# Another placement of the pair products in a CIN layer-1/layer-2 pipeline: steps 1, 6, 11, 16, 21, 26 and one group two tiles ahead

## The chip, the cores and the metric

The kernel runs on one core of one Trainium2 chip. The metric is the device time of one execution in microseconds (us). A core has five engines that run their own instruction streams and meet at semaphores: TensorE (PE, its weight loads are shown as PEld), VectorE (DVE), ScalarE (ACT), GpSimd (POOL) and SyncE (SP, which issues most DMAs here).

## The reference

For 1024 samples, 39 embedding rows of 16 numbers are gathered. Three layers of a compressed interaction network follow, and a small perceptron on their sums:

```
z   = einsum('bfd,bgd->bfgd', x0, xk).reshape(b, f * g, d)     # x0: 39 fields, xk: the layer before
cur = einsum('bpd,pm->bmd', z, W)                              # 128 outputs per layer, xk = cur
...
z = sum over d of the three cur, concatenated (384) and dense_ctx (16)
h = max(z @ W_top1 + b_top1, 0); h = max(h @ W_top2 + b_top2, 0); y = h @ W_top3
```

In layer 1 the pair (f, g) and the pair (g, f) share a product, so the kernel forms 20 shifted products of x with itself instead of 39 x 39.

## The kernel before, in words

**Tiles, blocks, quads.** The batch is cut into 32 tiles of 32 samples. A tile is 4 blocks of 8 samples (128 columns of sample x dimension). Four tiles make a quad, 8 quads in all: the first quad is written out, quads 1 to 6 are a hardware loop (`Fori`), and the last is written out. The four tiles of a quad are called the first to the fourth tile here (i = 0 to 3 in the code).

**Steps.** Each engine's program counts steps s = 0 to 39 in a tile, ten to a block (n = block, q = s % 10). In step s, PE makes one piece of layer 2 (`layer2_piece`: three matmuls, since fp32 is split in a high and a low part) in one of five PSUM banks (`pieces`). Pieces of even q are weighed by ACT (`weigh_piece`, four activations into `parts`), pieces of odd q by DVE (`sum_piece`, four, or three at q = 9, multiply-adds onto `parts`). PE may not reuse a bank before the piece of five steps earlier has been taken: step 10 waits for the DVE piece of step 5, and so on. When a block's 19 DVE multiply-adds are done, POOL adds its 20 partial sums in three instructions (`add_parts`: L342 over 1024 columns, L344 and L347 over 512), after the two or three gathers that its program has in front of them. DVE ends the addition one block later (`halve_tails` at q = 7, `finish_cur2` at q = 8).

**Layer 1 of the next tile.** It is put between these steps. It has seven groups k = 0 to 6 (`PAIRK`) per tile. For a group DVE multiplies `partners` by `x_rep` into one of two `pairs` buffers (`make_pairs`, L538, the product) at the step in `S_PAIR`. ACT takes the high part one step later (`take_pairs_high`, `S_HIGH`), DVE the low part two steps later (`take_pairs_low`, L554, `S_LOW`), and PE adds the group onto `cur1_bank` with three matmuls seven steps later (`sum_pairs`, L670 to L672, `S_SUM`). One and two steps after the last sum ACT and DVE take `cur1` out of PSUM (`copy_cur1_hi`, `take_cur1`). The product and the low part have all operands in SBUF; the multiply-adds of L528 read PSUM.

**Other work.** In the first and second tile of a quad PE also does layer 3 and the perceptron of the quad before (steps 25 to 55 of the quad). SP stores the gathered rows, loads `x_rep` and `partners` two tiles ahead and `x_diag` one tile ahead, in program order in one queue.

Of the kernel before, what the change touches and what calls it, by code (L numbers as in the profile page):

```python
# [32 lines left out]
TILES, BLOCKS = 4, 16  # L33
# [7 lines left out]
PAIRK = (SHIFTS + REP - 1) // REP  # L41
# [5 lines left out]
PIECES = 10  # L47
# [7 lines left out]

S_PAIR = [3 + 4 * k for k in range(PAIRK)]
S_HIGH = [x + 1 for x in S_PAIR]
S_LOW = [x + 2 for x in S_PAIR]  # L60
S_SUM = [x + 7 for x in S_PAIR]
S_G = [2, 12, 22, 32]
# [24 lines left out]
def cin_kernel(nc, t, out):  # L87

    ctx = ExitStack()
    with ctx:  # L90
# [291 lines left out]
        def _(act):  # L382
            def weigh_piece(u, n, q):

                g, i = u * BLOCKS + n, A_PIECES.index(q)
                k = g * len(A_PIECES) + i
                if i == 0:
                    wait(act, tree_done, (g - 1) * TREE)
                    act.wait_ge(x_cols_ready, u * TILES + n // 4 + 1)
                act.wait_ge(l2a_ready, k + 1)  # L390
                src = pieces[(n * PIECES + q) % BANKS]
                for r in range(4):
                    f = 4 * q + r
                    last = nc.scalar.activation(parts[n % 2][:, 4 * i + r, :], src[:, r * H:(r + 1) * H], ACT.Copy,  # L394
                                                scale=x_cols[n // 4][:, n % 4, f:f + 1])
                last.then_inc(prod_done, 1)
# [12 lines left out]
            def take_pairs_high(tile, i, k):  # L409
                g, buf, rows = tile * PAIRK + k, (i * PAIRK + k) % 2, rows_of(k)  # L410
                act.wait_ge(pairs_ready, g + 1)
                wait(act, pairs_used, g - 1)
                nc.scalar.activation(pairs_hi[buf][0:rows, :], pairs[buf][0:rows, :], ACT.Copy  # L413
                                     ).then_inc(pairs_hi_ready, 1)
# [45 lines left out]
            for part, cols in w1_raw:  # L460
                last = nc.scalar.activation(w1_hi[:, cols], part.rearrange("p f m -> p (f m)"), ACT.Copy)
# [12 lines left out]
            def quad(u, first, last):  # L474
                for i in range(TILES):
                    tile, more = u * TILES + i, not (last and i == TILES - 1)
                    for s in range(4 * PIECES):
                        n, q = 4 * i + s // PIECES, s % PIECES
                        if q in A_PIECES:
                            weigh_piece(u, n, q)  # L480
                        if more and s in S_HIGH:
                            take_pairs_high(tile + 1, i + 1, S_HIGH.index(s))
                        if more and s == S_X[i] + 1:
                            copy_x_cols(tile + 1, (i + 1) % TILES)
                        if s - 1 in (S_G_FIRST if i == 0 else S_G):
                            if n >= G_LAG:
                                copy_g(u, n - G_LAG)
                            elif not first:
                                copy_g(u - 1, BLOCKS + n - G_LAG)
                        at = 4 * PIECES * i + s  # L490
                        if not first:
                            if at == S_L3_COPY:
                                copy_l3(u - 1)
                            if at in S_RELU1:
                                relu1(u - 1, S_RELU1.index(at))
                            if at == S_RELU2:
                                relu2(u - 1)
                            if at - 1 == S_Y:
                                copy_y(u - 1)
                        if more and s == S_SUM[-1] + 1:  # L500
                            copy_cur1_hi(tile + 1, i + 1)
# [13 lines left out]
        def _(dve):  # L515
# [98 lines left out]
            def quad(u, first, last):  # L614
                for i in range(TILES):
                    tile, more = u * TILES + i, not (last and i == TILES - 1)
                    for s in range(4 * PIECES):
                        n, q = 4 * i + s // PIECES, s % PIECES
                        if q in D_PIECES:
                            sum_piece(u, n, q)  # L620
                        if q in (Q_HALVE, Q_FINISH):
                            step = halve_tails if q == Q_HALVE else finish_cur2
                            if n >= 2:
                                step(u, n - 2)
                            elif not first:
                                step(u - 1, BLOCKS + n - 2)
                        if more and s in S_PAIR:
                            make_pairs(tile + 1, i + 1, S_PAIR.index(s))
                        if more and s in S_LOW:
                            take_pairs_low(tile + 1, i + 1, S_LOW.index(s))  # L630
                        if more and s == S_SUM[-1] + 2:
                            take_cur1(tile + 1, (tile + 1) * TILE_B, i + 1)

# [242 lines left out]
```

## Time and profile before

| what | value |
|---|---|
| median of 3 runs (1337.85 to 1340.86) | 1338.43 us |
| profiled execution: its own time | 1340.8 us |
| profiled execution: span | 1339.0 us |
| granted TensorE clock, mean | 0.990 |
| PE busy | 1281.1 us, 96% of the span |
| DVE busy | 1149.6 us, 86% |
| POOL busy | 1058.3 us, 79% |
| ACT busy | 915.3 us, 68% |

The busy time of PE counts overlapping matmuls once, and the ends of matmuls are modelled, so 96% does not say by itself that PE sets the time. The shares are means over a quad whose four tiles are not alike.

### The profile page before, as it was taken

Reading aid. Unit: us, or ns where it says so; the run is one execution under the profiler, and the core shown is the slowest. Engines: PE = TensorE matmul, PEld = TensorE weight load, DVE = VectorE, ACT = ScalarE, POOL = GpSimd, SP = SyncE. Lnnn points to the kernel's source line nnn. Section 1 sums busy time; section 2 is a strip of 40 time slices with the busy share of each in tenths; the row PEclk is TensorE's granted clock in tenths of the full one; section 3 lists DMA queues with packets and bytes.
Section 4 is the critical chain, followed back from the end, with each engine's and each line's share of the span. In section 5 each row is a group of like instructions: output and inputs, shape, how many; then the busy total and the mean of one; then the engine's idle time right before and its main releaser. Section 6 shows DMA issues by size and latency. Waiting matters only on the chain. (4 is left out here: it accounts for less than half of the span.)

```text
span 1339.0 us, 25654 instructions
## 1 busy us (share of the span) xinstructions
PE 1281.1 (96%) x5983; PEld 1017.3 (76%) x5983; DVE 1149.6 (86%) x3210; ACT 915.3 (68%) x3053; POOL 1058.3 (79%) x743
## 2 busy tenths in 40 slices
PE   4899999999999999999999999999999999999998
PEld 2577777877788777887768877788767887788787
DVE  3499999699888999789986999969998699988983
ACT  2377776677666777577765777757776577766783
POOL 7588888688886888779887788868888688884561
PEclk9699999999999999999999999999999999999999
DMA  7623233322233322223332133330333322333000
GB/s 197 158 54 52 61 64 65 61 41 53 48 61 61 64 54 46 44 56 61 65 65 44 25 63 66 65 63 9 62 64 66 61 40 44 55 61 61 2 3 1
DMA packets 129470, 76.62 MB, mean 57 GB/s; under 512 B 90792, under 2 KB 98201, under 8 KB 129301
## 3 DMA queue, kind: packets, MB, share of 16 engines
q1 hardware_dynamic: 119061, 72.07, 26.5%
q0 software_dynamic: 10240, 2.64, 2.2%
q8 instruction: 64, 1.05, 0.3%
q14 instruction: 105, 0.86, 0.2%
HBM read 68.16 MB, written 3.87 MB: 54 GB/s over the span
## 5 line engine op out<-in xcount | busy, mean ns | idle before, releaser
L394 ACT ACTIVATE parts<-pieces,x_cols 128x128 f32<-128x128 f32 x2560 | 717.9, 377 | 188.3 <-PE pieces L690 159.4
L528 DVE SCALAR_TENSOR_TENSOR parts<-pieces,x_cols,parts 128x128 f32<-128x128 f32 x2432 | 678.7, 339 | 136.8 <-PE pieces L690 99.4
L688 PE MATMUL pieces<-w_hi,cur_hi 128*128 128x512 f32 (+1 forms) x1280 | 549.3, 429 | 29.2 <-DVE parts L528 23.0
L690 PE MATMUL pieces<-w_hi,cur_lo 128*128 128x512 f32 (+1 forms) x1280 | 499.4, 390 | 0.0
L689 PE MATMUL pieces<-w_lo,cur_hi 128*128 128x512 f32 (+1 forms) x1280 | 499.1, 390 | 0.0
L342 POOL TENSOR_TENSOR parts<-parts 128x1024 f32<-128x1024 f32 x127 | 324.2, 2553 | 149.8 <-DVE parts L528 144.4
L333 POOL DMA_INDIRECT emb<-in_table,rows x320 | 345.1, 1079 | 79.7 <-issue 60.9
L688 PEld LDWEIGHTS pieces<-w_hi,cur_hi 128*128 128x128 f32 x1280 | 242.1, 189 | 102.3 <-DVE parts L528 46.4
L690 PEld LDWEIGHTS pieces<-w_hi,cur_lo 128*128 128x128 f32 x1280 | 241.2, 188 | 51.7
L689 PEld LDWEIGHTS pieces<-w_lo,cur_hi 128*128 128x128 f32 x1280 | 242.3, 189 | 47.7
L413 ACT ACTIVATE pairs_hi<-pairs 117x512 fp32r<-117x512 f32 (+1 forms) x224 | 141.9, 634 | 190.9 <-DVE pairs L538 137.3
L538 DVE TENSOR_TENSOR pairs<-partners,x_rep 117x512 f32<-117x512 f32 (+1 forms) x217 | 207.2, 955 | 0.7 <-issue 0.7
L554 DVE TENSOR_TENSOR pairs_lo<-pairs,pairs_hi 117x512 fp32r<-117x512 f32 (+1 forms) x224 | 201.0, 897 | 6.1 <-issue 2.0
L344 POOL TENSOR_TENSOR parts<-parts 128x512 f32<-128x512 f32 x127 | 190.8, 1503 | 10.0
L347 POOL TENSOR_TENSOR tails<-parts 128x512 f32<-128x512 f32 x127 | 188.3, 1483 | 11.8
L670 PE MATMUL cur_bank<-pairs_hi,w_hi 117*128 117x512 f32 (+1 forms) x224 | 96.0, 429 | 3.0 <-DVE pairs_lo L554 1.1
L711 PEld LDWEIGHTS xbank<-G,w 128*128 128x128 f32 x624 | 83.1, 191 | 11.9 <-issue 5.2
L701 PE MATMUL gbank<-x_diag,cur 128*128 128x320 f32 x256 | 91.5, 439 | 0.0
L672 PE MATMUL cur_bank<-pairs_lo,w_hi 117*128 117x512 f32 (+1 forms) x224 | 90.0, 402 | 0.0
L671 PE MATMUL cur_bank<-pairs_hi,w_lo 117*128 117x512 f32 (+1 forms) x224 | 89.8, 401 | 0.0
L711 PE MATMUL xbank<-G,w 128*128 128x128 f32 x624 | 85.1, 275 | 1.8 <-ACT G L428 1.2
L670 PEld LDWEIGHTS cur_bank<-pairs_hi,w_hi 117*128 117x128 f32 (+1 forms) x224 | 42.6, 190 | 34.9 <-DVE pairs_lo L554 17.0
(66 smaller groups left out, 597.6 us busy)
## 6 DMA issues: line engine op xcount, KB each, us to landing
partners<-x_wide SPq DMA_DIRECT2D x62, 546.0 KB
partners<-x_wide SPq DMA_DIRECT2D x31, 468.0 KB
x_rep<-x_wide SPq DMA_DIRECT2D x96, 78.0 KB
emb<-in_table,rows POOLq DMA_INDIRECT x320
x_diag<-x_cols SPq DMA_DIRECT2D x256, 10.0 KB
x_wide<-emb SPq DMA_DIRECT2D x32, 80.0 KB
x_wide<-emb SPq DMA_DIRECT2D x32, 32.0 KB
wt<-in_wt SPq DMA_DIRECT2D x1, 1024.0 KB
```

The source lines that it names most:

```text
L333: pool.indirect_dma_start(emb[i % 2][:, j, :], None, t["table"], bass.IndirectOffsetOnAxis(ap=rows[i % 2][:, j:j + 1], axis=0)).then_inc(g ...
L342: pool.tensor_tensor(v[:, 0:8], v[:, 0:8], v[:, 8:16], ALU.add).then_inc(tree_done, 1)
L344: pool.tensor_tensor(v[:, 0:4], v[:, 0:4], v[:, 4:8], ALU.add).then_inc(tree_done, 1)
L347: pool.tensor_tensor(out4[:], v[:, 0:4], v[:, 16:20], ALU.add).then_inc(tree_done, 1)
L394: last = nc.scalar.activation(parts[n % 2][:, 4 * i + r, :], src[:, r * H:(r + 1) * H], ACT.Copy, scale=x_cols[n // 4][:, n % 4, f:f + 1])
L528: nc.vector.scalar_tensor_tensor(acc, src[:, r * H:(r + 1) * H], x_cols[n // 4][:, n % 4, f:f + 1], acc, ALU.mult, ALU.add).then_inc(acc_d ...
L538: nc.vector.tensor_tensor(pairs[buf][0:rows, :], partners[i % 2][0:rows, k, :], x_rep[i % 2][0:rows, :], ALU.mult).then_inc(pairs_ready, 1)
L554: nc.vector.tensor_tensor(pairs_lo[buf][0:rows, :], pairs[buf][0:rows, :], pairs_hi[buf][0:rows, :].bitcast(FP32), ALU.subtract).then_inc( ...
L688: nc.tensor.matmul(dst[:, 0:width], hi[:, cols], w1_hi[:, ws], start=True, stop=False)
L689: nc.tensor.matmul(dst[:, 0:width], hi[:, cols], w1_lo[:, ws], start=False, stop=False)
L690: nc.tensor.matmul(dst[:, 0:width], lo[:, cols], w1_hi[:, ws], start=False, stop=True).then_inc(l2d_ready if q in D_PIECES else l2a_ready, 1)
L711: last = nc.tensor.matmul(xbank[:, 0:P], w2[:, f, :], G[:, :, f, :], start=f == 0, stop=f == F - 1)
```

## The change

The first group of a tile is made two tiles ahead, in steps 37 to 39, and the other six are made in the tile before, every fifth step from step 1. The offsets of the high part, the low part and the sum stay +1, +2 and +7, so the sums go from steps 10, 14, ..., 34 to 4, 8, 13, 18, 23, 28, 33 (the first group's sum is 4 + 40 - 37 = 7 steps after its product, in the next tile). The number of instructions is the same.

```diff
-S_PAIR = [3 + 4 * k for k in range(PAIRK)]
+STEPS = 4 * PIECES
+S_PAIR = [37 - STEPS, 1, 6, 11, 16, 21, 26]
 S_HIGH = [x + 1 for x in S_PAIR]
 S_LOW = [x + 2 for x in S_PAIR]
 S_SUM = [x + 7 for x in S_PAIR]
...
+                    more2 = not (last and i >= TILES - 2)
...
+                        if first and i == 0 and s == S_PAIR[1]:
+                            make_pairs(1, 1, 0)
                         if more and s in S_PAIR:
                             make_pairs(tile + 1, i + 1, S_PAIR.index(s))
+                        if more2 and s - STEPS == S_PAIR[0]:
+                            make_pairs(tile + 2, i + 2, 0)
...
```

ACT's `take_pairs_high` and DVE's `take_pairs_low` get the same two extra conditions.

Two places of DVE's program show what moves. The first is block 1 of a third tile (its multiply-adds are the rows with `x_cols2`; `pieces4` with x3 is the last piece of a block, step 9 or 19, `pieces1` the first, step 11). Before:

```order
L528 SCALAR_TENSOR_TENSOR parts0<-pieces4,x_cols2,parts0 128x128 x3
L554 TENSOR_TENSOR pairs_lo0<-pairs0,pairs_hi0 117x512
L528 SCALAR_TENSOR_TENSOR parts1<-pieces1,x_cols2,parts1 128x128 x4
L538 TENSOR_TENSOR pairs1<-partners1,x_rep1 117x512
L528 SCALAR_TENSOR_TENSOR parts1<-pieces3,x_cols2,parts1 128x128 x4
L554 TENSOR_TENSOR pairs_lo1<-pairs1,pairs_hi1 117x512
L528 SCALAR_TENSOR_TENSOR parts1<-pieces0,x_cols2,parts1 128x128 x4
L538 TENSOR_TENSOR pairs0<-partners1,x_rep1 117x512
L528 SCALAR_TENSOR_TENSOR parts1<-pieces2,x_cols2,parts1 128x128 x4
L582 TENSOR_TENSOR tails1<-tails1 128x256
L554 TENSOR_TENSOR pairs_lo0<-pairs0,pairs_hi0 117x512
L588 TENSOR_TENSOR cur2_1<-tails1 128x128
```

And in the changed kernel (its lines are six further down: L534, L544 and L560 are L528, L538 and L554 of before):

```order
L534 SCALAR_TENSOR_TENSOR parts0<-pieces4,x_cols2,parts0 128x128 x3
L534 SCALAR_TENSOR_TENSOR parts1<-pieces1,x_cols2,parts1 128x128 x4
L544 TENSOR_TENSOR pairs0<-partners1,x_rep1 117x512
L534 SCALAR_TENSOR_TENSOR parts1<-pieces3,x_cols2,parts1 128x128 x4
L560 TENSOR_TENSOR pairs_lo0<-pairs0,pairs_hi0 117x512
L534 SCALAR_TENSOR_TENSOR parts1<-pieces0,x_cols2,parts1 128x128 x4
L544 TENSOR_TENSOR pairs1<-partners1,x_rep1 117x512
L534 SCALAR_TENSOR_TENSOR parts1<-pieces2,x_cols2,parts1 128x128 x4
L588 TENSOR_TENSOR tails1<-tails1 128x256
L594 TENSOR_TENSOR cur2_1<-tails1 128x128
L560 TENSOR_TENSOR pairs_lo1<-pairs1,pairs_hi1 117x512
```

The low part that stood between two blocks is gone from there, so the first piece of a block follows the last piece of the block before at once, and a product follows that first piece. Before, block 1 had five product or low-part instructions between two block ends; now it has four.

The second place is the end of a third tile and the start of the fourth (`x_cols3`). Before:

```order
L528 SCALAR_TENSOR_TENSOR parts1<-pieces2,x_cols2,parts1 128x128 x4
L582 TENSOR_TENSOR tails1<-tails1 128x256
L588 TENSOR_TENSOR cur2_1<-tails1 128x128
L528 SCALAR_TENSOR_TENSOR parts1<-pieces4,x_cols2,parts1 128x128 x3
L528 SCALAR_TENSOR_TENSOR parts0<-pieces1,x_cols3,parts0 128x128 x4
L528 SCALAR_TENSOR_TENSOR parts0<-pieces3,x_cols3,parts0 128x128 x4
L538 TENSOR_TENSOR pairs0<-partners0,x_rep0 117x512
L528 SCALAR_TENSOR_TENSOR parts0<-pieces0,x_cols3,parts0 128x128 x4
```

And in the changed kernel:

```order
L534 SCALAR_TENSOR_TENSOR parts1<-pieces2,x_cols2,parts1 128x128 x4
L588 TENSOR_TENSOR tails1<-tails1 128x256
L544 TENSOR_TENSOR pairs0<-partners0,x_rep0 117x512
L594 TENSOR_TENSOR cur2_1<-tails1 128x128
L534 SCALAR_TENSOR_TENSOR parts1<-pieces4,x_cols2,parts1 128x128 x3
L560 TENSOR_TENSOR pairs_lo0<-pairs0,pairs_hi0 117x512
L534 SCALAR_TENSOR_TENSOR parts0<-pieces1,x_cols3,parts0 128x128 x4
L544 TENSOR_TENSOR pairs1<-partners0,x_rep0 117x512
L534 SCALAR_TENSOR_TENSOR parts0<-pieces3,x_cols3,parts0 128x128 x4
L560 TENSOR_TENSOR pairs_lo1<-pairs1,pairs_hi1 117x512
L534 SCALAR_TENSOR_TENSOR parts0<-pieces0,x_cols3,parts0 128x128 x4
```

Up to the piece of step 5 (the last row) four instructions stand where one stood.

## Rows read from the trace of the kernel before

**Rows 1.** Page, part 5: line, engine, form, count, busy us, mean ns.

```profile
L538 DVE TENSOR_TENSOR pairs<-partners,x_rep 117x512 f32<-117x512 f32 (+1 forms) x217 | 207.2, 955 | 0.7 <-issue 0.7
```

**Rows 2.** Windows, tiles 3, 4, 2 of quad 2: us, PE, PEld, DVE, ACT, POOL busy.

```profile
447.50:483.50 36.00, 35.53 (x154) 27.63 (x154) 35.16 (x101) 27.54 (x95) 31.94 (x23) 1.00 0.31 60
483.50:522.05 38.55, 35.88 (x155) 27.42 (x154) 37.88 (x108) 28.50 (x97) 33.90 (x26) 1.00 0.30 58
407.00:447.50 40.50, 40.50 (x207) 33.52 (x205) 33.62 (x95) 29.84 (x102) 32.01 (x20) 1.00 0.25 50
```

**Rows 3.** Waits of PE, then of DVE, 447.5 to 522 us: total, times, longest.

```profile
PE pieces L688 <- DVE parts L528: 1.2, 3, 0.6
...
DVE parts L528 <- PE pieces L690: 0.4, 1, 0.4
```

**Rows 4.** Timeline of DVE, third and fourth tile: start us, us, instruction.

```profile
449.16 1.90 DVE L528 SCALAR_TENSOR_TENSOR parts<-pieces,x_cols,parts 128x128 f32<-128x128 f32 x7
...
452.17 1.35 DVE L538 TENSOR_TENSOR pairs<-partners,x_rep 117x512 f32<-117x512 f32 x1
...
457.39 0.85 DVE L528 SCALAR_TENSOR_TENSOR parts<-pieces,x_cols,parts 128x128 f32<-128x128 f32 x3
458.17 0.68 DVE L554 TENSOR_TENSOR pairs_lo<-pairs,pairs_hi 117x512 fp32r<-117x512 f32 x1
458.99 1.13 DVE L528 SCALAR_TENSOR_TENSOR parts<-pieces,x_cols,parts 128x128 f32<-128x128 f32 x4 [0.15 <-ACT parts L394]
460.04 1.69 DVE L538 TENSOR_TENSOR pairs<-partners,x_rep 117x512 f32<-117x512 f32 x1
...
462.69 0.74 DVE L554 TENSOR_TENSOR pairs_lo<-pairs,pairs_hi 117x512 fp32r<-117x512 f32 x1
...
467.24 0.85 DVE L528 SCALAR_TENSOR_TENSOR parts<-pieces,x_cols,parts 128x128 f32<-128x128 f32 x3
...
469.65 1.93 DVE L554 TENSOR_TENSOR pairs_lo<-pairs,pairs_hi 117x512 fp32r<-117x512 f32 x1
...
485.21 3.08 DVE L528 SCALAR_TENSOR_TENSOR parts<-pieces,x_cols,parts 128x128 f32<-128x128 f32 x11
488.21 2.39 DVE L538 TENSOR_TENSOR pairs<-partners,x_rep 117x512 f32<-117x512 f32 x1
```

**Rows 5.** Timeline of POOL, the same stretch: starts of L342.

```profile
450.58 2.40 POOL L342 TENSOR_TENSOR parts<-parts 128x1024 f32<-128x1024 f32 x1 [0.24 <-issue]
...
458.77 2.40 POOL L342 TENSOR_TENSOR parts<-parts 128x1024 f32<-128x1024 f32 x1
...
468.60 2.42 POOL L342 TENSOR_TENSOR parts<-parts 128x1024 f32<-128x1024 f32 x1
...
478.02 2.79 POOL L342 TENSOR_TENSOR parts<-parts 128x1024 f32<-128x1024 f32 x1 [0.84 <-DVE parts L528]
...
487.65 2.41 POOL L342 TENSOR_TENSOR parts<-parts 128x1024 f32<-128x1024 f32 x1 [0.24 <-issue]
```

**Rows 6.** Timeline of DVE and PE where the loop turns (quad 2 to 3).

```profile
521.99 0.86 DVE L528 SCALAR_TENSOR_TENSOR parts<-pieces,x_cols,parts 128x128 f32<-128x128 f32 x3
525.45 2.16 DVE L528 SCALAR_TENSOR_TENSOR parts<-pieces,x_cols,parts 128x128 f32<-128x128 f32 x8 [2.60 <-issue]
...
529.96 0.73 DVE L554 TENSOR_TENSOR pairs_lo<-pairs,pairs_hi 117x512 fp32r<-117x512 f32 x1
...
530.09 0.50 PE L688 MATMUL pieces<-w_hi,cur_hi 128*128 128x512 f32 x1 [0.44 <-DVE parts L528]
...
530.89 0.40 PE L670 MATMUL cur_bank<-pairs_hi,w_hi 117*128 117x512 f32 x1
...
531.59 0.40 PE L688 MATMUL pieces<-w_hi,cur_hi 128*128 128x512 f32 x1
```

**Rows 7.** Timeline of SP, and a window with its DMA share, GB/s.

```profile
531.11 1.33 SPq L278 DMA_DIRECT2D partners<-x_wide  x3
...
542.00:546.00 4.00, 4.00 (x17) 2.64 (x15) 4.00 (x11) 3.15 (x12) 3.69 (x3) 1.00 0.10 13
```

More of the change, by code:

```diff
@@ L480, in quad @@
                             weigh_piece(u, n, q)
+                        if first and i == 0 and s == S_HIGH[1]:
+                            take_pairs_high(1, 1, 0)
                         if more and s in S_HIGH:
                             take_pairs_high(tile + 1, i + 1, S_HIGH.index(s))
+                        if more2 and s - STEPS == S_HIGH[0]:
+                            take_pairs_high(tile + 2, i + 2, 0)
                         if more and s == S_X[i] + 1:
@@ L616, in quad @@
                     tile, more = u * TILES + i, not (last and i == TILES - 1)
+                    more2 = not (last and i >= TILES - 2)
                     for s in range(4 * PIECES):
@@ L626, in quad @@
                                 step(u - 1, BLOCKS + n - 2)
+                        if first and i == 0 and s == S_PAIR[1]:
+                            make_pairs(1, 1, 0)
                         if more and s in S_PAIR:
                             make_pairs(tile + 1, i + 1, S_PAIR.index(s))
+                        if more2 and s - STEPS == S_PAIR[0]:
+                            make_pairs(tile + 2, i + 2, 0)
+                        if first and i == 0 and s == S_LOW[1]:
+                            take_pairs_low(1, 1, 0)
                         if more and s in S_LOW:
                             take_pairs_low(tile + 1, i + 1, S_LOW.index(s))
+                        if more2 and s - STEPS == S_LOW[0]:
+                            take_pairs_low(tile + 2, i + 2, 0)
                         if more and s == S_SUM[-1] + 2:
```

## The prediction

> **What bounds the kernel now.** The page gives PE 96% and DVE 86% of the span, which reads as a PE-bound kernel. I went on to windows of one tile each, because the tiles of a quad are not alike. In the second tile PE is busy without a gap, 40.50 of 40.50 us, and DVE only 33.62. In the third DVE is busy 35.16 of 36.00 us, and in the fourth 37.88 of 38.55 [rows 2]. So PE sets the time in the first two tiles, where it also has layer 3 and the perceptron, and DVE sets it in the last two. The list of waits agrees: PE waits there for DVE's pieces, 1.2 us at three places in the list, and DVE waits for PE just once, 0.4 us [rows 3]. The reader is to see that PE's waits in these tiles are not bubbles that a smoother schedule removes. DVE has 0.84 + 0.67 = 1.5 us of idle time in two tiles, and a new order of the same instructions can gain no more than this, unless it makes them shorter.
>
> They can become shorter or longer. A product or low part takes 0.68 us when nothing disturbs it [rows 4], but the mean of the product is 955 ns [rows 1]. The timelines of DVE and POOL side by side show where the rest comes from. The product at 460.04 takes 1.69 us; POOL's L342 runs from 458.77 to 461.17, and the product ends 0.56 us after that. The same holds for the low part at 469.65 (1.93 us; L342 from 468.60), the product at 452.17 (1.35 us; from 450.58) and the one at 488.21 (2.39 us; from 487.65) [rows 4, 5]. Write "into" for how far L342 has run when the DVE instruction starts. Into is 1.27, 1.05, 1.59 and 0.56 us, and the loss over 0.68 is 1.01, 1.25, 0.67 and 1.71. Loss plus into is 2.26 to 2.30 each time. So DVE is held until L342 ends, and **loss = 2.28 - into**. Instructions that come later in the block find POOL in step with them and lose little (0.74 us at 462.69, so 0.06). A bound tile pays three such losses, 2.9 us in the third tile and 4.0 in the fourth. L342 itself starts when block sum and gathers allow: 0.52 us after the block's last piece (457.39 + 0.85 = 458.24), 0.51 after that of 467.24, and 1.6 after the last piece at a tile's end (first three of the eleven at 485.21, so about 486.07) [rows 4, 5]. At 478.02 POOL had waited 0.84 us for DVE, so that block's L342 starts as soon as DVE lets it.
>
> The Trainium skill ("SBUF — State Buffer", section "Who interferes with whom") says that a DVE instruction with two SBUF inputs and a GpSimd one that reads SBUF exclude each other, and that the second to issue blocks until the first is done. By that rule a hit at into 0.64 costs 2.40 - 0.64 = 1.76 us where my line gives 1.64; over some 30 hits the sum below would be about 4 us higher. The rule speaks against a product right behind a block's start.
>
> **The change part by part.**
> *Where the hits fall.* Before, a low part or product stood between the block's last piece and the next block's first one, so L342 was already 1.27 or 1.05 us on its way when the next SBUF instruction came. Now the first piece follows at once and a product follows it. The piece takes 460.04 - 458.99 = 1.05 us, and DVE no longer has to wait there for ACT's 0.15 [rows 4].
> - Block 1 of a fourth tile: L342 still 0.5 behind the block end; into 1.05 - 0.5 = 0.55 to 0.65, loss about 1.64, before 1.01: +0.6.
> - Block 2: the same, before 1.25: +0.4.
> - Block 0 of a fourth tile: the moved low part (0.62 start to start) and the first piece put the product 1.67 us after the block end, L342 comes at 1.6 to 1.8. I take it that the product just goes first; the low part, 0.62 + 1.05 later, then meets L342 and loses (1.8 + 0.35 + 2.28) - 3.35 = 1.1, before 1.71: -0.6. (L342 was lengthened from 2.40 to 2.79 by such a meeting at 478.02 [rows 5], hence 0.35.) If L342 goes first, it is 2.2, so +0.5.
> - Third tile: block 0: DVE comes 0.60 + 0.62 us later, into about 1.6 as before, 0. Block 1: POOL now has to wait for DVE, into 0.95, loss 1.33, +0.3. Block 2: +0.4.
> Together +0.4 in a fourth and +0.7 in a third tile.
> *What smoothing gives back.* Each of blocks 0 to 2 now has four SBUF instructions instead of up to five. PE's lead of five banks then hides more, and of DVE's idle time the wait for PE (0.4) and one ACT wait (0.15) can go: -0.5 per quad. The rest stays, being short gaps.
> *The first tile of a quad.* The product and low part of steps 37 to 39 are now DVE's last work before the loop turns. DVE then sits idle 2.60 us (521.99 + 0.86 to 525.45) with nothing named but issue, and the step-5 piece ends at 530.0, just as PE starts step 10 at 530.09 after 0.44 us of waiting [rows 6]. DVE now turns 1.25 us later and has one more SBUF instruction before step 5 (0.62): +1.9. PE meanwhile also has more to do before step 10, the sums of steps 4 and 8 at 531.59 - 530.89 = 0.70 us each. It would reach step 10 at 529.65 + 1.4 = 531.05, DVE allows 531.9: a wait of 0.85 against 0.44, +0.4. The later product in block 1 adds 0.3, before layer 3 gives DVE room. Sum +0.7.
> *Costs at nothing.* In the rest of the first tile and in the second, hits grow too, but PE covers 40.50 - 33.62 = 6.9 us. The data of the group two tiles ahead is there: SP issues the partners at 531.1, the traffic has died down by 542 to 546 (13 GB/s) [rows 7], and step 37 of that tile comes some 20 us later; were this cover gone, it would cost that delay. No DMA moves and SP's queue has the same order. ACT waits for the products as before and has over 7 us idle per tile. PE has the same 21 sum matmuls.
>
> **Sum.** Quads 1 to 6: 0.4 + 0.7 - 0.5 + 0.7 = 1.3 us each, 7.8. Quad 7 has pairs in three tiles, about 1.0. Quad 0 has no second job for PE, so three of its tiles are bound by DVE: 0.4 less a share of idle time, about 1 in all. That is +10 us on the profiled 1340.8, 1350.8. The profiled execution is 2.4 above the median, so I forecast 1338.4 + 9.8 = 1348 us.
>
> **The rivals.**
> *Smoothing wins* (faster). If L342 starts over 1.05 us after the block end, the product of blocks 1 and 2 slips in ahead of it and only the low part is hit, losing about 1.0. The three losses are then 1.0, 1.0 and 1.1, so -0.9 in a fourth tile and 0 in a third, and with the idle time all gained -1.5 more: -2.4 + 0.5 for the turn, -1.9 per quad; over seven quads -13, and -2 in quad 0. That gives 1323. Should only the idle time be gained and the hits stay, it is -1.5 x 7 = -10, 1328. For it: PE's waits on DVE are real, POOL is busy 31.94 us in the third tile, and adding issue gaps it is nearly full, so it may fall behind. Against: it starts at 0.5 or less in every block but the last. Chance 0.26, 1322 to 1335.
> *Nothing changes.* The group moved to step 37 only changes its place in DVE's fixed sum of work; extra losses and regained idle time cancel. 1336 to 1341. For it: the terms are small and of both signs. Chance 0.18.
> *The turn of the loop decides* (slower than forecast). If the 1.9 us at the turn is not covered by the two sums, because PE has to wait for the low part itself, or if the product after L39 meets L342 in block 0 in all tiles (+1.1 instead of -0.6), quads cost 1.2 to 1.7 more: about +9 on the forecast, 1353 to 1362. Chance 0.10.
> *The forecast*, lock losses outweigh the smoothing, own range 1341 to 1353: chance 0.46.
>
> **How the numbers follow.** About 0.2% (2.7 us) is what a measurement can tell. Faster is the first rival, 0.26. Within 0.2% is the second less its upper edge, 0.17. Slower is the forecast and the third, 0.57. The range leaves out the lower half of the first rival's results and the upper part of the third: 1328 to 1358.
>
> **What the profile of the changed kernel would show.** The products of steps 11 and 21 at 2.2 to 2.4 us in third and fourth tiles, one to two tenths of a microsecond on the mean of the product; the product of step 1 at 0.68 or over 2.5 us; PE's first long wait in those tiles at step 18; after a turn of the loop, step 10 waiting for about 0.9 us; windows of third tiles at 36 to 36.5 us. If instead these products read 0.68 us with L342 starting later, the first rival holds. The forecast is wrong above all if POOL's phase to DVE is not what the old order gave, since all the lock terms are differences of a few tenths between two engines that wait for each other.

## The result, and the profile after

| what | before | after |
|---|---|---|
| median | 1339.26 us (4 runs) | 1392.73 us (4 runs, 1391.5 to 1394.0) |
| ratio, 95% interval | | 1.0399 (1.0381 to 1.0417) |
| profiled span | 1339.0 us | 1389.7 us |
| mean clock granted to TensorE | 0.990 | 0.982 |

The change costs 53 us. I had forecast 10, with a range up to 1358: the direction was right and the size was off by a factor of five. (The median of before here has one run more than the table ahead of the prediction.)

The profiled spans differ by 50.7 us. I cut both traces at PE's first layer 2 matmul of each tile and took differences. "Forecast" is the term of the prediction for the same stretch.

| stretch | before | after | difference | forecast |
|---|---|---|---|---|
| up to the end of the very first tile | 89.0 | 94.0 | +5.0 | with the next row |
| other three tiles of quad 0 | 110.7 | 114.9 | +4.2 | +1 for the quad |
| a quad of the loop, mean of six | 160.5 | 166.8 | +6.3, six times +37.7 | +1.3, six times 7.8 |
| its first tile | 45.4 | 48.8 | +3.4 | +0.7 |
| its second tile | 40.7 | 40.7 | 0 | 0 |
| its third tile | 36.0 | 37.8 | +1.8 | +0.7 |
| its fourth tile | 38.4 | 39.5 | +1.1 | +0.4 |
| gained by smoothing, per quad | | | nothing seen | -0.5 |
| quad 7 and the end | 176.3 | 180.2 | +3.8 | +1.0 |

**The low parts and products.** The page of after (line, engine, form, count, busy us, mean ns) answers to [rows 1]:

```profile
L544 DVE TENSOR_TENSOR pairs<-partners,x_rep 117x512 f32<-117x512 f32 (+1 forms) x217 | 251.7, 1160 | 5.3 <-issue 5.3
...
L560 DVE TENSOR_TENSOR pairs_lo<-pairs,pairs_hi 117x512 fp32r<-117x512 f32 (+1 forms) x224 | 180.2, 805 | 8.5 <-ACT pairs_hi L414 8.5
```

The product grew from 955 to 1160 ns, 5 above the upper end of what I had named (one to two tenths of a microsecond). The low part got shorter, from 897 to 805. Together they take 431.9 us; before they took 408.2, so DVE works 24 us longer in all. That is less than half of the 53.

**The tiles of quad 2**, windows with the columns of [rows 2], first to fourth tile:

```profile
375.63:424.70 49.07, 45.94 (x232) 37.61 (x233) 36.51 (x100) 27.12 (x92) 34.23 (x26) 0.97 0.27 49
424.70:465.38 40.68, 40.68 (x206) 33.58 (x205) 33.74 (x95) 29.86 (x103) 30.01 (x20) 1.00 0.24 50
465.38:503.19 37.81, 35.94 (x154) 27.45 (x154) 36.72 (x101) 27.18 (x95) 33.57 (x23) 1.00 0.29 57
503.19:543.13 39.94, 36.09 (x154) 27.33 (x154) 39.06 (x109) 28.27 (x98) 35.10 (x26) 1.00 0.29 55
```

The second tile is covered by PE, as before. In the third DVE is busy 36.72 us where it was 35.16 [rows 2], +1.56, and its idle time is 1.09 us where it was 0.84. So smoothing gave nothing back: the idle time rose. The first tile is the surprise. DVE is idle 12.6 us there and PE 3.1, so neither engine fills it, and yet it is 3.4 us longer on average.

**The third tile, DVE and then POOL** (start us, us, instruction), to be read as [rows 4, 5]; L343, L345 and L348 are POOL's three additions, L342, L344 and L347 of before:

```profile
470.19 0.68 DVE L544 TENSOR_TENSOR pairs<-partners,x_rep 117x512 f32<-117x512 f32 x1
...
471.82 1.87 DVE L560 TENSOR_TENSOR pairs_lo<-pairs,pairs_hi 117x512 fp32r<-117x512 f32 x1
...
479.55 2.35 DVE L544 TENSOR_TENSOR pairs<-partners,x_rep 117x512 f32<-117x512 f32 x1
...
489.39 2.31 DVE L544 TENSOR_TENSOR pairs<-partners,x_rep 117x512 f32<-117x512 f32 x1
```

```profile
470.22 2.91 POOL L343 TENSOR_TENSOR parts<-parts 128x1024 f32<-128x1024 f32 x1 [0.24 <-ACT parts L395]
...
478.92 2.42 POOL L343 TENSOR_TENSOR parts<-parts 128x1024 f32<-128x1024 f32 x1
...
488.75 2.40 POOL L343 TENSOR_TENSOR parts<-parts 128x1024 f32<-128x1024 f32 x1
```

L343 runs 478.92 to 481.34 and the product that starts at 479.55 ends at 481.90, 0.56 us later. Into is 0.63 and the loss 1.67, sum 2.30: the line from the trace of the kernel before holds at the new place. The product of step 1 slips in ahead of L343 and takes 0.68, and the low part behind it pays 1.19 (forecast 1.1).

**What PE waits for** (waited for: us in total, times, longest), whole run:

```profile
PE pieces L703 <- DVE parts L534: 29.9, 43, 1.9
...
PE cur_bank L685 <- DVE pairs_lo L560: 13.8, 15, 7.8
PE xbank L726 <- ACT G L429: 13.8, 6, 2.3
```

In the kernel before, the first row was 23.0 us over 34 times, and the last one was this (L711 and L428 are L726 and L429 of after):

```profile
PE xbank L711 <- ACT G L428: 1.2, 6, 0.3
```

L726 is PE's layer 3, L429 is ACT's copy of `G`, the operand of layer 3, out of PSUM. I had not looked at it. In the first tile of quad 2, DVE, ACT and PE around step 25, with POOL's addition that holds the product:

```profile
400.21 2.40 POOL L343 TENSOR_TENSOR parts<-parts 128x1024 f32<-128x1024 f32 x1
...
400.84 2.33 DVE L544 TENSOR_TENSOR pairs<-partners,x_rep 117x512 f32<-117x512 f32 x1
...
403.21 0.63 ACT L414 ACTIVATE pairs_hi<-pairs 117x512 fp32r<-117x512 f32 x1 [2.71 <-DVE pairs L544]
403.74 0.42 ACT L429 ACTIVATE G<-gbank 128x320 f32<-128x320 f32 x1
...
404.48 0.93 PE L726 MATMUL xbank<-G,w 128*128 128x128 f32 x6 [2.31 <-ACT G L429]
```

ACT's program has the high part of step 22 in front of the copy of `G` at step 23. The high part waits 2.71 us for the product of step 21, which POOL's L343 holds for 2.33 us instead of 0.68. The copy, which waits for nothing of that product, comes late with it, and PE stands still for 2.31 us in a tile where it is the bound. This repeats in each loop quad.

**The turn of the loop**, quad 2 to 3, where [rows 6] stood, PE and DVE:

```profile
543.13 0.79 PE L703 MATMUL pieces<-w_hi,cur_hi 128*128 128x512 f32 x1 [2.18 <-issue]
...
543.65 0.68 DVE L560 TENSOR_TENSOR pairs_lo<-pairs,pairs_hi 117x512 fp32r<-117x512 f32 x1
548.34 1.13 DVE L534 SCALAR_TENSOR_TENSOR parts<-pieces,x_cols,parts 128x128 f32<-128x128 f32 x4 [4.01 <-ACT parts L395]
```

DVE is idle 4.01 us (3.8 to 4.3 in the five turns; before 2.5 to 3.2), and comes back 5.1 to 5.8 us after PE's first matmul of the quad, where it was 2.9 to 3.9. PE is idle at the turn too, 1.9 to 2.2 us before its first matmul (before 1.6 to 1.9).

**The start.** In the very first tile the extra group is made in steps 1 to 3, for a sum in step 4:

```profile
59.33 1.29 DVE L544 TENSOR_TENSOR pairs<-partners,x_rep 117x512 f32<-117x512 f32 x2 [5.26 <-issue]
...
62.32 0.79 PE L685 MATMUL cur_bank<-pairs_hi,w_hi 117*128 117x512 f32 x1 [7.83 <-DVE pairs_lo L560]
```

PE waits 7.83 us for it. All kernels below with POOL's additions whole and this extra group end their first tile at 93.2 to 95.8 us, the kernel before at 89.0. The 7.83 us are not all the group's: the kernel before has a wait of 6.0 us in this tile, for ACT. And the first product that reads `partners` starts at 58.7 to 61.0 us in every kernel profiled here, with or without the extra group, though the tile starts anywhere from 41.0 to 50.8 us. Counted from that product, the rest of the tile takes 30.2 us in the kernel before and 34.5 to 36.4 us with the group. So a group that early costs 4 to 6 us once.

### The profile page after: what moved, and what is told of

It is laid out like the page before. It is cut to its first block and busy times, and to the rows that moved or that the text cites. A ratio compares the mean times of both kernels' runs of the same rounds, so it can differ in the third digit from the quotient of the medians.

```text
span 1389.7 us, 25660 instructions
## 1 busy us (share of the span) xinstructions
PE 1296.2 (93%) x5983; PEld 1021.5 (74%) x5983; DVE 1174.4 (85%) x3210; ACT 907.3 (65%) x3053; POOL 1056.6 (76%) x743
## 5 line engine op out<-in xcount | busy, mean ns | idle before, releaser
L395 ACT ACTIVATE parts<-pieces,x_cols 128x128 f32<-128x128 f32 x2560 | 707.0, 382 | 183.3 <-PE pieces L705 164.8
L534 DVE SCALAR_TENSOR_TENSOR parts<-pieces,x_cols,parts 128x128 f32<-128x128 f32 x2432 | 675.8, 340 | 146.6 <-PE pieces L705 107.1
L703 PE MATMUL pieces<-w_hi,cur_hi 128*128 128x512 f32 (+1 forms) x1280 | 554.7, 433 | 38.9 <-DVE parts L534 29.9
L343 POOL TENSOR_TENSOR parts<-parts 128x1024 f32<-128x1024 f32 x127 | 313.8, 2471 | 202.1 <-DVE parts L534 184.6
L334 POOL DMA_INDIRECT emb<-in_table,rows x320 | 351.6, 1099 | 79.7 <-issue 65.6
L544 DVE TENSOR_TENSOR pairs<-partners,x_rep 117x512 f32<-117x512 f32 (+1 forms) x217 | 251.7, 1160 | 5.3 <-issue 5.3
L345 POOL TENSOR_TENSOR parts<-parts 128x512 f32<-128x512 f32 x127 | 192.5, 1516 | 10.0
L348 POOL TENSOR_TENSOR tails<-parts 128x512 f32<-128x512 f32 x127 | 188.8, 1487 | 11.8
L560 DVE TENSOR_TENSOR pairs_lo<-pairs,pairs_hi 117x512 fp32r<-117x512 f32 (+1 forms) x224 | 180.2, 805 | 8.5 <-ACT pairs_hi L414 8.5
L685 PE MATMUL cur_bank<-pairs_hi,w_hi 117*128 117x512 f32 (+1 forms) x224 | 93.2, 416 | 13.9 <-DVE pairs_lo L560 13.8
L726 PEld LDWEIGHTS xbank<-G,w 128*128 128x128 f32 x624 | 84.9, 194 | 26.8 <-issue 19.9
L726 PE MATMUL xbank<-G,w 128*128 128x128 f32 x624 | 86.9, 279 | 16.4 <-ACT G L429 13.8
L716 PE MATMUL gbank<-x_diag,cur 128*128 128x320 f32 x256 | 94.9, 452 | 0.4 <-ACT G L429 0.4
L685 PEld LDWEIGHTS cur_bank<-pairs_hi,w_hi 117*128 117x128 f32 (+1 forms) x224 | 42.9, 191 | 39.4 <-DVE pairs_lo L560 25.1
## 6 DMA issues: line engine op xcount, KB each, us to landing
wt<-in_wt SPq DMA_DIRECT2D x1, 1024.0 KB, 13.8
```

The source lines that it names most:

```text
L334: pool.indirect_dma_start(emb[i % 2][:, j, :], None, t["table"], bass.IndirectOffsetOnAxis(ap=rows[i % 2][:, j:j + 1], axis=0)).then_inc(g ...
L343: pool.tensor_tensor(v[:, 0:8], v[:, 0:8], v[:, 8:16], ALU.add).then_inc(tree_done, 1)
L345: pool.tensor_tensor(v[:, 0:4], v[:, 0:4], v[:, 4:8], ALU.add).then_inc(tree_done, 1)
L348: pool.tensor_tensor(out4[:], v[:, 0:4], v[:, 16:20], ALU.add).then_inc(tree_done, 1)
L534: nc.vector.scalar_tensor_tensor(acc, src[:, r * H:(r + 1) * H], x_cols[n // 4][:, n % 4, f:f + 1], acc, ALU.mult, ALU.add).then_inc(acc_d ...
L544: nc.vector.tensor_tensor(pairs[buf][0:rows, :], partners[i % 2][0:rows, k, :], x_rep[i % 2][0:rows, :], ALU.mult).then_inc(pairs_ready, 1)
```

## The experiments

My theory (A in most expectations) is that POOL's additions hold the products and low parts at their new places, and that what stands behind a held product is late with it, ACT's copy of `G` above all. The rivals: the order costs the same without POOL; the late copy hides another limit; the group made two tiles ahead is what costs; the distance of five steps is. Times are medians, ratios are to runs of the kernel before on the same chip. "Tiles" are the means of the four tiles in quads 1 to 6: before 45.4, 40.7, 36.0, 38.4, after 48.8, 40.7, 37.8, 39.5.

### How much needs POOL: before_short_pool, after_short_pool

Each of POOL's three additions is made over 128 columns only, so both kernels leave out most of the sum and compute something else; both also clear `tails` once at the start. The edit is the same in both (one line of three shown):

```diff
-                pool.tensor_tensor(v[:, 0:8], v[:, 0:8], v[:, 8:16], ALU.add).then_inc(tree_done, 1)
+                pool.tensor_tensor(v[:, 0:1], v[:, 0:1], v[:, 8:9], ALU.add).then_inc(tree_done, 1)
```

> The kernel before with POOL's three additions cut to one column group of 128 each (most of the sum over the parts is left out, so this computes another result); DVE's and PE's programs are untouched. With next to nothing on POOL that can hold DVE, products and low parts should read 0.68 us everywhere. Expected by the lock theory: the third tile shrinks by its 2.9 us of losses, down to what PE allows (34.5), in all 15 to 25 us faster than before, 1315 to 1323.

> The changed kernel with the same cut of POOL's additions. Lock theory: all three losses (third and fourth tiles, wait for G at step 25) come from products held by POOL, so the difference to the kernel before with the same cut is small, under 10 us of the 53. If the order by itself costs (DVE's end of tile, the turn of the loop, PE waiting for the sums), the difference stays at 30 us or more.

Measured: 1300.61 us (0.9702, 0.967 to 0.9733) with the old order, below what I expected, and 1316.95 us (0.9823, 0.9795 to 0.9852) with the new one. Page of after_short_pool (lines two further down):

```profile
L562 DVE TENSOR_TENSOR pairs_lo<-pairs,pairs_hi 117x512 fp32r<-117x512 f32 (+1 forms) x224 | 152.7, 682 | 7.5 <-ACT pairs_hi L416 7.5
...
L546 DVE TENSOR_TENSOR pairs<-partners,x_rep 117x512 f32<-117x512 f32 (+1 forms) x217 | 149.1, 687 | 8.9 <-issue 8.9
```

On average every product and low part is back at 0.68 us, and none takes over 0.9, so it is POOL's additions that hold them. The new order then costs 16.3 us, not 53.5: some 37 us need POOL's additions. The 16 are more than the 10 I had expected at most. In the traces they are 2.5 us up to the end of the first tile and 2.0 per loop quad, of which the turn and the first tile have 0.9 and the fourth tile 0.8. Most of these 0.8 are PE's own idle time at the turn of the loop, before its first matmul of a quad: 1.3 to 1.5 us with the old order, 2.0 to 2.3 with the new one, and none where a quad is reached without a turn.

### ACT copies G first: g_first_b

```diff
+                        if s in (S_G_FIRST if i == 0 else S_G) and s != S_G_FIRST[-1]:
+                            if n >= G_LAG:
+                                copy_g(u, n - G_LAG)
...
                         if more and s in S_HIGH:
                             take_pairs_high(tile + 1, i + 1, S_HIGH.index(s))
```

> The changed kernel with one edit on ACT alone: the copy of G (steps 2, 12, 22, 32) goes ahead of the high part that stands in the same step, not one step behind it. Theory A (queue on ACT): in the first tile of a quad ACT holds the last copy of G behind a high part that waits for the late product of step 21, and PE waits 2.4 us for it at step 25, where it waited 0.4 before. Then this edit gives back 2 us in 7 quads, about 14 us: 1379. Theory B (locks alone): DVE is late by as much whatever ACT copies first, and the time stays within 3 us of 1393.

Measured: 1374.47 us (1.026, 1.0243 to 1.0277). Theory A holds. Its list of waits no longer has a row in which layer 3 waits for `G`; the first tile falls from 48.8 to 46.4 us, and the others stay (40.7, 37.8, 39.4). So 18 of the 53 us were the copy of `G` queued behind a held high part. Nothing else changed but the place of these copies in ACT's program.

### The group two tiles ahead at a distance of four steps: early_spacing4_b

```diff
-S_PAIR = [37 - STEPS, 1, 6, 11, 16, 21, 26]
+S_PAIR = [37 - STEPS, 3, 7, 11, 15, 19, 23]
```

(The extra group of the very first tile goes to steps 1, 2 and 3, here and in every kernel below that has no other product at step 1.)

> The changed kernel with products at steps 3, 7, 11, 15, 19, 23 (every fourth step again), the first group still two tiles ahead at step 37. Theory A (the phases of the products to POOL's additions cost, the group two tiles ahead does not): the third and fourth tiles go back to about 36 and 36.6 us plus the turn, the wait for G to 0.4: 1338 to 1346. Theory C (the group at step 37 itself costs, through the turn of the loop and DVE's end of tile): at least half of the loss stays, 1365 or more.

Measured: 1336.98 us in 10 runs (0.9975, 0.9965 to 0.9984), tiles 45.1, 40.7, 35.4, 37.9. It is a hair faster than the kernel before, though it pays the 6 us at the start and has DVE idle 3.9 to 4.4 us at the turn. So a kernel with the group two tiles ahead need not be slower. That the group by itself costs nothing does not follow, and the next run shows that it costs something. Here DVE's idle time in the third tile fell from 0.8 to 0.5 us, so the smoothing that I had booked can happen.

### One group moved and nothing else: one_moved

```diff
-S_PAIR = [37 - STEPS, 1, 6, 11, 16, 21, 26]
+S_PAIR = [37 - STEPS, 7, 11, 15, 19, 23, 27]
```

> One part of the change alone: only the first group goes to steps 37 to 39 two tiles ahead; the other six stay at 7, 11, ..., 27, as in the kernel before. In the very first tile the extra group is made at steps 1, 2 and 3. Theory A (the group two tiles ahead costs only at the turn of the loop, about 1 us per quad, and takes the product of step 3 away from POOL's L342, which gives about as much back; what the change costs comes from the places of the other six): 1333 to 1343 us, no difference beyond 0.3%. Rival (the group at the end of a tile is itself what costs, 2 us per quad or more): 1352 us or more. The first tile should last 45 to 46 us, the third 35 to 36, DVE idle 3.8 to 4.4 us at the turn.

Measured: 1353.69 us (1.0104, 1.0085 to 1.0123), outside theory A's range, and in that of the rival. By the trace neither is right: 6.1 us are lost up to the end of the first tile, which I had not put in, and a loop quad costs 1.0 us, half of what the rival says, 0.7 of it in the fourth tile (45.6, 40.7, 36.1, 39.1). The product of step 3 is gone from POOL's way, and in the fourth tile that of step 7 stands there instead, and that of step 11 is held longer:

```profile
499.60 1.77 DVE L544 TENSOR_TENSOR pairs<-partners,x_rep 117x512 f32<-117x512 f32 x1
...
504.14 2.61 DVE L544 TENSOR_TENSOR pairs<-partners,x_rep 117x512 f32<-117x512 f32 x1
```

Before they took 0.68 and 1.70 us, and the product of step 3 in front of them 2.39. In the fourth tile, taking a product out of an addition's way did not take the loss away. In the third tile the loss of step 3 did go (the 14 products and low parts take 12.0 us, before 12.7 to 12.8), but the tile is no shorter: DVE's idle time rose from 0.8 to 1.2 us. So this part of the change alone costs 13 us, 6 of them once at the start.

### Out of the way of two hits: two_moved

```diff
-S_PAIR = [37 - STEPS, 1, 6, 11, 16, 21, 26]
+S_PAIR = [37 - STEPS, 1, 6, 13, 16, 23, 26]
```

> The changed kernel with two of its six products moved: 11 to 13 and 21 to 23 (high parts, low parts and sums with them, two steps later); all else as in the change. Phase theory: these two products then start a piece later and after L342 has run 1.7 us or more, so each loses at most 0.6 where it loses 1.65, and the high part of step 24 no longer stands ahead of G's copy. Third tiles 37.8 to about 36, G's wait 2.4 to 0.4, per quad -5: 1350 to 1360. If spacing or the group two tiles ahead is the cause, 1380 or more.

Measured: 1372.87 us (1.0238, 1.022 to 1.0256), tiles 46.3, 40.7, 37.8, 39.3: what g_first_b gives, and no more, outside my range of 1350 to 1360. The wait for `G` is gone, since no high part stands at step 22, but the third tile stays at 37.8. DVE, then POOL, in block 1 of a third tile:

```profile
476.33 1.31 DVE L544 TENSOR_TENSOR pairs<-partners,x_rep 117x512 f32<-117x512 f32 x1
...
479.27 1.78 DVE L544 TENSOR_TENSOR pairs<-partners,x_rep 117x512 f32<-117x512 f32 x1
```

```profile
474.68 2.41 POOL L343 TENSOR_TENSOR parts<-parts 128x1024 f32<-128x1024 f32 x1
...
478.88 1.62 POOL L348 TENSOR_TENSOR tails<-parts 128x512 f32<-128x512 f32 x1
```

The product at 476.33 loses 0.63 us to L343. The next, at 479.27, meets the third addition, L348, which ends at 480.50, and ends 0.55 later at 481.05: it loses 1.10. Together 1.73, where the one product of step 11 lost 1.67 in the changed kernel. My line was right, but I had written it for the first addition only. **Every product or low part that is held ends 0.54 to 0.56 us after the POOL addition it met, whichever of the three it is**; this is so for all 92 that took over 0.9 us in the kernel before and all 96 in the changed one.

### The same distance of five, two steps later: phase3, two_later_b

First phase3, then two_later_b:

```diff
-S_PAIR = [37 - STEPS, 1, 6, 11, 16, 21, 26]
+S_PAIR = [37 - STEPS, 3, 8, 13, 18, 23, 26]
```

> Products at 3, 8, 13, 18, 23 and 26: as the variant with all six two steps later, but the last group keeps its steps, so the take of layer 1 stays at step 35. In that variant PE waited 1.8 us at the start of tiles for it. Theory A (phase, plus that late take): third tiles near 36, no wait at step 0: 1335 to 1350. If spacing 5 by itself is bad: 1370 or more.

```diff
-S_PAIR = [37 - STEPS, 1, 6, 11, 16, 21, 26]
+S_PAIR = [37 - STEPS, 3, 8, 13, 18, 23, 28]
```

> The changed kernel with its six products two steps later: 3, 8, 13, 18, 23, 28, the first group still at 37. Spacing 5 as in the change, other phase. A product then starts two pieces (2.1 us) after a block end, so L342 has 0.9 us or less to run: loss 0.7 instead of 1.65 in blocks 1 and 2, and the high part of step 24 stands behind the copy of G. Theory A (phase): 1335 to 1348. Theory D (any spacing of 5 with the group ahead is bad, because DVE has no time left to catch up before the tile ends): 1375 or more.

Measured: phase3 1360.17 us (1.0148, 1.0131 to 1.0165), tiles 45.6, 40.7, 37.4, 38.9; two_later_b 1377.06 us (1.0284, 1.0254 to 1.0313), tiles 46.0, 42.7, 37.8, 38.0. Both missed my range, and two_later_b lies in that of the rival, the distance of five. In phase3 three products are still held in most third tiles (1.9, 1.8 and 1.8 us), and DVE is idle for 1.7 us there, twice as long as before. The tile grew by 1.4 us, of which the idle time is 0.9 and the products and low parts 0.5: most of it is not the length of the hits. In two_later_b the 14 products and low parts of a third tile take 11.4 to 13.0 us, about what they took before (12.8) or less, but the last sum stands at step 35 and `cur1` is taken at the tile's end. PE then waits for it at step 0:

```profile
PE pieces L703 <- DVE cur_lo L567: 30.5, 20, 2.3
```

That row is not in the list of before. The second tile, until then 40.7 in all kernels, is 2 us longer by it. So this kernel says little about a distance of five steps: it has an edge of its own. phase3, without that edge, lies between my range and the rival's 1370, and leaves the rival open in part.

### The turn of the loop: turn33_b, not_over_turn

turn33_b makes the group four steps earlier and keeps its sum at step 4:

```diff
-S_PAIR = [37 - STEPS, 1, 6, 11, 16, 21, 26]
+S_PAIR = [33 - STEPS, 1, 6, 11, 16, 21, 26]
...
-S_SUM = [x + 7 for x in S_PAIR]
+S_SUM = [4] + [x + 7 for x in S_PAIR[1:]]
```

> The changed kernel with the group two tiles ahead made at steps 33 to 35 instead of 37 to 39 (its sum stays at step 4). The loop then turns behind a layer-2 piece on DVE as before. Theory T (the low part as last instruction lengthens DVE's turn from 2.6 to 3.2 us to 4.0 and puts it 1.2 us later): 5 turns give back 1 to 2 us each, 1383 to 1388. If the turn does not matter: 1391 to 1395.

not_over_turn makes no such group in the fourth tile, but one in each first tile, at steps 1 to 3 (DVE's product shown):

```diff
-                    more2 = not (last and i >= TILES - 2)
+                    more2 = not (last and i >= TILES - 2) and i < TILES - 1
...
-                        if first and i == 0 and s == S_PAIR[1]:
-                            make_pairs(1, 1, 0)
+                        if i == 0 and s == S_PAIR[1]:
+                            make_pairs(tile + 1, 1, 0)
```

> The changed kernel, but the fourth tile of a quad makes no group two tiles ahead; the first tile of every quad makes that group at step 1 beside the other one, as the change does in quad 0. DVE then turns the loop behind a layer-2 piece. Theory T: DVE's idle time at the turn falls from 4.0 to about 2.7 us, but two products stand in front of step 3, so DVE is late again there: net 0 to -4, 1389 to 1393. The trace's idle time at the turn is what tells; a total below 1385 would say that the turn costs more than the profile shows.

Measured: turn33_b 1392.61 us (1.0378, 1.0353 to 1.0403), not_over_turn 1404.15 us (1.0475, 1.0457 to 1.0492). In both DVE's idle time at the turn falls, to 2.4 to 2.8 and 2.5 to 3.3 us. So it is the group at the tile's end, with its low part as DVE's last instruction, that makes the turn longer for DVE. Whether that is because the low part waits for ACT's high part was not tested by itself. But neither gains. In turn33_b the product and low part of steps 33 and 35 delay `cur1`, and PE waits for it (10.7 us in the list, 13 times). In not_over_turn the sum of step 4 needs a low part that DVE makes only after the turn:

```profile
PE cur_bank L685 <- DVE pairs_lo L560: 38.1, 16, 9.6
```

The first tile is 50.5 us long. Making this group before the turn is the lesser evil.

### Clear of the first addition, in twos: clear_of_l342, clear_g_first

```diff
-S_PAIR = [37 - STEPS, 1, 6, 11, 16, 21, 26]
+S_PAIR = [37 - STEPS, 3, 7, 13, 17, 23, 27]
```

> Products at 3, 7, 13, 17, 23, 27 and the first group at 37 two tiles ahead: in blocks 1 and 2 no product or low part before the second piece of the block, so L342 should be over or nearly. Phase theory: losses only at step 3; third tile down to 34.6 to 35 us (what PE allows), fourth by 1.5 to 2: 15 to 22 us faster than the kernel before, 1318 to 1326. If POOL's start moves with DVE so that the loss only changes place: 1333 to 1340.

> The order of clear_of_l342 (1322.7 us) with ACT's copies of G ahead of the high parts, as in g_first. In clear_of_l342 PE does not wait for G, so if the copies only cost where PE waits for them, as in the changed kernel, nothing is gained here: 1320 to 1325 us. Rival (the copies of G set the length of the first tile in some other way, for instance through the cur3 pieces behind them): 1 us less per quad, 1316 us or below.

Measured: 1322.68 us (0.9871, 0.9853 to 0.9888), 1.3% faster than the kernel before and 70 us faster than the changed one, with the group two tiles ahead and the same instructions. With ACT's copies of `G` first as well it is 1322.61 us (0.9874, 0.9853 to 0.9896): no difference, since PE does not wait for `G` here. Tiles 45.1, 40.7, 34.8, 37.0. The page, a window of a third tile, and DVE and POOL in it:

```profile
L544 DVE TENSOR_TENSOR pairs<-partners,x_rep 117x512 f32<-117x512 f32 (+1 forms) x217 | 199.6, 920 | 6.3 <-issue 6.3
...
L560 DVE TENSOR_TENSOR pairs_lo<-pairs,pairs_hi 117x512 fp32r<-117x512 f32 (+1 forms) x224 | 157.7, 704 | 8.2 <-ACT pairs_hi L414 8.1
```

```profile
442.06:476.87 34.81, 34.81 (x155) 28.09 (x154) 33.76 (x101) 27.37 (x95) 31.59 (x23) 1.00 0.33 62
```

```profile
454.32 2.16 DVE L534 SCALAR_TENSOR_TENSOR parts<-pieces,x_cols,parts 128x128 f32<-128x128 f32 x8 [0.15 <-ACT parts L395]
456.40 0.68 DVE L544 TENSOR_TENSOR pairs<-partners,x_rep 117x512 f32<-117x512 f32 x1
...
464.63 1.91 DVE L544 TENSOR_TENSOR pairs<-partners,x_rep 117x512 f32<-117x512 f32 x1
```

```profile
454.09 2.42 POOL L343 TENSOR_TENSOR parts<-parts 128x1024 f32<-128x1024 f32 x1
...
463.57 2.40 POOL L343 TENSOR_TENSOR parts<-parts 128x1024 f32<-128x1024 f32 x1
```

In this third tile only two of the 14 products and low parts are held, 0.95 us long at step 3 and 1.91 at 464.63. While L343 runs, from 454.09 to 456.51, DVE has eight multiply-adds to do, which read PSUM and are not held. The product comes when 0.11 us of the addition are left and takes 0.68. In the next block POOL issues three gathers instead of two, L343 starts 9.48 us after the one before, and the product at 464.63 is caught (1.91). Products and low parts take 357.3 us in all, 51 less than before, and PE has no idle time left in the third tile: PE is the bound there now.

## Why the prediction was right or wrong

**What bounds the kernel: right, and not carried through.** The first two tiles belong to PE and the last two to DVE. But I used "PE covers it" and "ACT has over 7 us idle per tile" to set all later effects in PE's own tiles to nothing. The step that failed is *Costs at nothing*, in its sentence that ACT waits for the products as before. Idle time on ACT in a tile says nothing about the place where it lies. Of the queue rows I should have read: ACT's program has `S_G` = 2, 12, 22, 32, copied one step later, and the new high parts stand at 2, 7, 12, 17, 22, 27, so at step 22 the copy waits behind a high part whose product is held. This missing term is 18 us, shown by g_first_b, about 2.4 in each quad from quad 1 on.

**Where the hits fall: right in the fourth tile, short in the third.** With the line "loss = 2.28 - into" I forecast 1.1 for the low part of block 0 (measured 1.18 to 1.19) and 2.2 to 2.4 us for the products of steps 11 and 21 (2.31 to 2.35). The fourth tile's 14 products and low parts grew from 13.8 to 14.3 us, forecast +0.4. In the third they grew from 12.8 to 14.3, forecast +0.7. In block 0 I took no change; there the product ran beside L343 and lengthened it to 2.91 us, so the low part came out at 1.87 against the 1.35 of before's product. In block 1 I took into for 0.95 because POOL would have to wait for DVE; it was 0.63.

**What smoothing gives back: wrong.** I booked 0.5 us per quad. DVE's idle time in a third tile rose from 0.8 to 1.1 us. It fell to 0.5 in early_spacing4_b, at a distance of four steps, but rose to 1.2 in one_moved, at the same distance, and to 1.7 in phase3, at five. So the distance alone does not set it, and I can't say what does. So third and fourth tile together cost 2.8 us per quad instead of 0.6, some 14 us more over the six loop quads and quad 7.

**The turn of the loop: right in kind, a little low.** Without the 2.4 us for `G` the first tile grew by 1.0; I had 0.7. I had the turn 1.25 us later for DVE; its return came about 2 us later against PE, and turn33_b ties the longer idle time to the group at the tile's end. That PE's own idle time at the turn would grow I had not put in.

**Quad 0: wrong.** I had +1 and it was +9.2. The extra group in the very first tile costs 5.0, with PE waiting 7.8 us where it waited 6.0 in the kernel before; I had given the group no term there. The quad's other three tiles, bound by DVE throughout, lose 4.2: their product of step 1 is held for 2.89 us, where that of step 3 took 2.4 to 2.6.

**The sum of the miss.** The traces differ by 50.7 us where I had 9.8: 17 for `G` (2.4 in seven quads), 14 in the third and fourth tiles, 8 in quad 0 and 2 in the rest of the first tiles, together 41.

**The rivals.** "Smoothing wins" fell in this kernel because L343 never started late enough. Its idea, an SBUF instruction that slips past the first addition, is what clear_of_l342 uses, and there it brings 1.3%. "The turn of the loop decides" named a real term, but not of this size: with POOL's additions short, the first tile (0.9 us per quad), PE's idle time at the turn (0.6) and the start (2.5 once) make about 12 of the 16 us.

**What stays open.** Why the losses in a block added up to the same 1.7 us in two_moved and in the changed kernel, while they fell in clear_of_l342, is read from the two traces and was not tested by moving POOL's gathers, which set when L343 starts. Whether the distance of five steps costs something beyond the hits is open too: no kernel at that distance came below 1360 us, and the idle time of phase3 speaks for it. The 5.26 us that DVE waits before its first products of quad 0 are marked only as issue. The code waits there for the loads of `x_rep` and `partners`, and that this product starts at 58.7 to 61.0 us in all kernels speaks for a load, but none was moved to test it. Why PE is idle longer at the turn with the new order is not shown either.

The Trainium skill ("SBUF — State Buffer", section "Who interferes with whom") says that the second to issue is blocked until the first is done. The traces agree that the second is held, but the held product or low part ends 0.55 us after the addition, and not 0.68 us after it, which is its time alone; so my line priced a hit better than the rule. The multiply-adds, whose one operand is in PSUM, were never held: 339 and 340 ns on average in the two kernels, 354 at most.

## What to carry to other kernels

Where two engines shut each other out, draw both timelines side by side and move the sensitive instructions to where the other engine does something else. Price a move against all instructions of the other engine, since a hit that is avoided on one may fall on the next. And when an instruction is going to be late, read on in the program of each engine that waits for it: what is queued behind it there, though it needs nothing of it, was the largest single loss of this change. An engine's idle share does not cover that.

## What the runs showed of the hardware that was not expected

- A product or low part (both operands in SBUF) that meets a POOL addition ends 0.54 to 0.56 us after it, for additions over 1024 and over 512 columns alike (188 cases in two kernels). The same line holds near the end: starting 0.2 us or less before the addition's end costs nothing or up to 0.08 us.
- POOL is held by DVE in the same way. An addition that starts while a DVE instruction with both operands in SBUF is running gets longer by what is left of that instruction, less 0.12 to 0.17 us (all 393 cases in two kernels in which over 0.2 us were left). The product at 470.19 had 0.65 us to go when L343 started, and L343 took 2.91 instead of 2.40 us. Additions over 512 columns take 1.30 us with only multiply-adds beside them, and 1.60 to 1.65 us behind a held product or low part.
- A turn of the hardware loop leaves DVE idle 2.5 to 3.2 us and PE 1.6 to 1.9 us in the kernel before, and 3.8 to 4.3 and 1.9 to 2.2 us in the changed one, whose last DVE instruction there is a low part. PE is not idle at all where a quad is reached without a turn.
